# Head steps every 12 tiles and own products every 5 tiles in the second gather stage

## The reference

```python
xn = layernorm(x)
# graph part: mean of the neighbours' rows, and the node's own row
agg  = segment_sum(xn[nbr], dst);  mean = agg / max(count, 1)
gnn  = xn @ W1.T + b1 + mean @ W2.T + b2
# mixing part: 8 heads of 32 columns
k = headnorm(xn) * kw + kb;  v = headnorm(xn) * vw + vb      # std with ddof=1
kv = einsum('nd,ne->de', k, v) / N                            # per head
mix = xn_heads @ kv + xn
x = x + gnn + mix
# experts: top-1 routing with a capacity, two matmuls with relu, scattered back
x = x + ffn(layernorm(x))
```

## Time and profile before

| | |
|---|---|
| median of 3 runs | 2139.8 us (2136.44 to 2140.73) |
| the profiled execution | 2139.9 us, span 2138.3 us |
| busy: PE / DVE / ACT / POOL | 75% / 65% / 34% / 48% of the span |
| 880 gathers on POOL (L439) | 894.3 us busy |
| `experts`, last block | from about 1671 us on |

### The profile page before, as it was taken

How to read it: one execution, slowest core, us unless ns; L and a number is a source line. 1 busy time by engine, 2 the same in 40 slices (tenths; PEclk the granted TensorE clock), 3 DMA queues, 4 the chain that set the end, 5 groups by cost and what they waited for, 6 DMA issues and landing times. The chain is left out here.

```text
span 2138.3 us, 26245 instructions
## 1 busy us (share of the span) xinstructions
PE 1593.7 (75%) x6551; PEld 889.5 (42%) x6551; DVE 1387.2 (65%) x4056; ACT 721.3 (34%) x2020; POOL 1036.1 (48%) x1021
## 2 busy tenths in 40 slices
PE   4666887677878777365555658888676699999997
PEld 3552332233333333022222224554365466666665
DVE  7568998789999998366656555555465144444444
ACT  3336997004877776000000001111064122222221
POOL 2001001777777777777777777777425111111111
PEclk9788999767999999555555557667555799999999
DMA  5117000333333333933333344444844422222200
GB/s 167 40 40 295 31 0 15 100 101 96 94 97 97 99 97 99 99 110 103 103 101 103 102 114 130 123 121 128 102 155 168 133 89 89 97 92 92 91 23 5
DMA packets 89183, 210.70 MB, mean 99 GB/s; under 512 B 20627, under 2 KB 49849, under 8 KB 86081
## 3 DMA queue, kind: packets, MB, share of 16 engines
q0 software_dynamic: 51888, 138.08, 24.8%
q1 hardware_dynamic: 35496, 70.56, 9.7%
q10 hardware_dynamic: 1680, 0.67, 0.2%
HBM read 163.98 MB, written 49.89 MB: 100 GB/s over the span
## 5 line engine op out<-in xcount | busy, mean ns | idle before, releaser
L902 DVE TENSOR_TENSOR XA<-XA,bank 128x257 f32 x880 | 369.0, 419 | 345.0 <-PE bank L657 319.5
L439 POOL DMA_INDIRECT G<-xn_parts,idx x440 | 443.0, 1007 | 277.7 <-DVE srcl L994 143.9
L439 POOL DMA_INDIRECT w<-xn_parts,idx x440 | 451.3, 1026 | 134.1 <-issue 134.1
L656 PE MATMUL bank<-G,S 128*128 128x257 f16 x440 | 154.8, 352 | 165.2 <-DMA G<-xn_parts,idx 140.4
L1582 POOL DMA_INDIRECT out<-ob,tok x64 | 66.6, 1040 | 401.7 <-DVE ob L1568 399.0
L656 PE MATMUL bank<-w,S 128*128 128x257 f16 x440 | 152.6, 347 | 138.8 <-DMA w<-xn_parts,idx 124.0
L529 ACT ACTIVATE LV<-LH,v 125x128 f16<-125x128 f16 x600 | 182.9, 388 | 189.5 <-DVE LH L1063 189.2
L1506 PE MATMUL bank<-w,ht 128*117 128x256 f32 (+1 forms) x1024 | 223.7, 379 | 0.0
L1495 PE MATMUL bank<-xt,w 128*128 128x468 f32 (+1 forms) x512 | 215.3, 579 | 0.8 <-ACT xt L1520 0.8
L1506 PEld LDWEIGHTS bank<-w,ht 128*117 128x117 f32 (+1 forms) x1024 | 188.8, 186 | 30.5 <-issue 0.4
L1530 ACT ACTIVATE ht<-bank,b1c 128x468 f32<-128x468 f32 (+1 forms) x128 | 85.7, 670 | 333.8 <-PE bank L1495 333.8
(11 more groups left out here) (225 smaller groups left out, 2542.9 us busy)
## 6 DMA issues: line engine op xcount, KB each, us to landing
w<-f SPq DMA_DIRECT2D x16, 1024.0 KB, 7.4
expert_rows<-G SPq DMA_DIRECT2D x7, 2048.0 KB, 21.3
xb<-expert_rows SPq DMA_DIRECT2D x8, 1028.0 KB, 11.4
xb<-expert_rows SPq DMA_DIRECT2D x8, 939.7 KB
G<-xn_parts,idx POOLq DMA_INDIRECT x440, 2.8
w<-xn_parts,idx POOLq DMA_INDIRECT x440, 2.8
XA<-x SPq DMA_DIRECT2D x6, 1024.0 KB, 5.7
xn_parts<-G POOLq DMA_DIRECT2D x12, 512.0 KB, 3.7
```

Of the source, the lines that this page charges most:

```text
L439: pool.indirect_dma_start(g[:, o:o + 2 * D], None, tab, bass.IndirectOffsetOnAxis(ap=idx[:, t:t + 1], axis=0)).then_inc(s_g[t % RING], 16)
L656: pe.matmul(psA[t % AR][:, 0:AGW], lhs, g[:, o + D:o + 2 * D + 1], start=True, stop=True)
L902: v.tensor_tensor(XA[:, ds(o, AGW)], XA[:, ds(o, AGW)], psA[t % AR][:, 0:AGW], ALU.add).then_inc(s_ev, 1)
```

## The change

The work and its order on each engine are the same; the tiles that it stands behind differ. Head steps come every `HS` = 12 tiles from tile 16 on, with VectorE's steps behind tiles s = 0 to 9 of the twelve as before, and TensorE's six pieces in two halves, three behind s = 10 and three behind s = 11. `KV_AT` and `OWN0` are now counted in tiles: 16 + 12 x 17 = 220. Own products start every `OS` = 5 tiles, with the transposes behind tile 0 and the matmuls behind tile 2 of the five; the last starts at tile 460, and VectorE's last add for it stands behind tile 465.

```diff
--- before.py
+++ after.py
@@ -77,9 +77,11 @@
 
 T0 = CHUNKS[0][3]
 COLS0, COLS1 = CHUNKS[0][1], CHUNKS[1][1]
-HEAD0, KV_AT = 1, 1 + NB // HD + 1
+HS, OS = 12, 5
+HEAD0 = GR
+KV_AT = HEAD0 + HS * (NB // HD + 1)
 OWN0 = KV_AT
-assert len(CHUNKS) == 2 and OWN0 * GR + 4 * NB < CHUNKS[1][3] and NB % LD == 1 and COLS1 % LB == 0
+assert len(CHUNKS) == 2 and OWN0 + OS * NB < CHUNKS[1][3] and NB % LD == 1 and COLS1 % LB == 0
 
 
 RB0, RB1 = 2, 4
@@ -741,8 +743,8 @@
         for h in range(2):
             pe.matmul(psG[h][:, 0:KW], zero32[:, :], W1[:, 0:KW], start=True, stop=False, skip_group_check=True)
         for t in range(T0, TILES):
-            g, s = (t - T0) // GR, (t - T0) % GR
-            if g == KV_AT and s == 0:
+            u = t - T0
+            if u == KV_AT:
                 for h in range(2):
                     ins = pe.matmul(psG[h][:, 0:KW], zero32[:, :], W1[:, 0:KW], start=False, stop=True,
                                     skip_group_check=True)
@@ -754,13 +756,16 @@
                               stop=True).then_inc(s_se, 1)
                 pe.wait_ge(s_kv, 1)
             sum_tile(t)
-            if HEAD0 <= g < KV_AT and s >= 10:
-                m, pieces = g - HEAD0, (HD if g - HEAD0 < NB // HD else 1) * 2
-                if s == 10:
+            m, s = (u - HEAD0) // HS, (u - HEAD0) % HS
+            if HEAD0 <= u < KV_AT and s >= HS - 2:
+                pieces = (HD if m < NB // HD else 1) * 2
+                if s == HS - 2:
                     pe.wait_ge(s_kn, m + 1)
-                products(m, range(min(s - 10, pieces), min(s - 9, pieces)), pieces - 1)
-            if OWN0 <= g and s % 2 == 0 and (g - OWN0) * LD + s // 4 < NB:
-                own((g - OWN0) * LD + s // 4, s % 4)
+                half = pieces // 2
+                products(m, range(0, half) if s == HS - 2 else range(half, pieces), pieces - 1)
+            b, s = (u - OWN0) // OS, (u - OWN0) % OS
+            if OWN0 <= u and s in (0, 2) and b < NB:
+                own(b, s)
 
     @block.vector
     def _(v):
@@ -1158,14 +1163,15 @@
             v.tensor_tensor(XA[:, xcols(b)], XA[:, xcols(b)], xr[b % LD], ALU.add).then_inc(s_x0, 1)
 
         for t in range(T0, TILES):
-            g, s = (t - T0) // GR, (t - T0) % GR
-            if g == KV_AT and s == 0:
+            u = t - T0
+            if u == KV_AT:
                 key_values()
             tile(t)
-            if HEAD0 <= g < KV_AT and s < 10:
-                heads(g - HEAD0, s, HD if g - HEAD0 < NB // HD else 1)
-            b = (g - OWN0) * LD + s // 4 - 1
-            if OWN0 <= g and s % 4 == 0 and 0 <= b < NB:
+            m, s = (u - HEAD0) // HS, (u - HEAD0) % HS
+            if HEAD0 <= u < KV_AT and s < HS - 2:
+                heads(m, s, HD if m < NB // HD else 1)
+            b, s = (u - OWN0) // OS - 1, (u - OWN0) % OS
+            if OWN0 <= u and s == 0 and 0 <= b < NB:
                 own(b)
```

## The result

The changed kernel took 2148.3 us in the median of 16 runs (2141.06 to 2154.85), beside 2139.4 us for the kernel before in the same session (16 runs). The ratio is 1.0042, with a 95% interval from 1.0029 to 1.0055: slower by 0.4%, about 9 us. The profiled execution has a span of 2151.4 us against 2138.3. It took 2153.1 us, 4.7 above the median of its kernel, while the one before (2139.9) lies on its median, so the two profiles are 13.1 us apart and the medians 8.9.

A forecast was written before the change was run, and what follows sets the result against it. GpSimd's issue of 880 gathers was taken to bound both gather stages, with transfers setting the tail. Terms -0.5 (x loads) + 0 (key-value step) + 2.7 (heads) + 4.4 (own products) = +6.6 us gave 2146 us, range 2133 to 2158.

The forecast's parts named there:

- What bounds the kernel: Both gather stages: issuing 880 gathers on GpSimd sets their length, the other engines work in its shadow; transfers set the tail.
- Own products out of the tail: End of the second gather stage: six blocks' products leave the last 24 tiles, worth nothing to the end.
- The term for the x loads: Tail of the second gather stage: moving the x loads out gives -0.5 us, bounds 0 and -1.3.
- Key-value step: Moved from tile 288 to tile 220, it holds TensorE 5.6 us at the sum and costs the same: 0.
- Heads in 12 tiles: Head stage: lumps of three pieces put VectorE out of phase, more gathers lengthened; +2.7 us, bounds -0.5 and +6 (+12 with jitter).
- Own products in 5 tiles: Tiles 220 to 460: L881 goes through all five places, 30 x 0.49 us against 10.3; +4.4 us, bounds 0 and +12.5.
- The sum: Whole kernel: -0.5 + 0 + 2.7 + 4.4 = +6.6 us, forecast 2146 us.
- The signs named beforehand: GpSimd gaps at most 0.31 us; gathers over 0.98 us (head), about 1.01 (own); last sum about 15 us behind last issue.
- C: Rival, faster: the tail is TensorE's, so removing products there takes 11.6 us off, 2128 us; chance 0.07.
- D: Rival, faster: with period 5 most L881 fall free at 0.15 us each, own stage loses 4.5, 2133.5 us; chance 0.13.
- E: Rival, slower: the ring fills, GpSimd stops and own products show at 0.5 us per block, +25 us, 2165 us; chance 0.05.
- B: Rival, no change: collisions keep their rate per L881 or are unrelated to VectorE; 2139.3, up to 2144 us; chance 0.27.

## Why the prediction was right, point by point

- **What bounds the kernel.** Right, and shown: GpSimd has no gap over 0.31 us in the profile after, and in the old schedule taking 43 us out of the gathers' lengths and 13 out of the tail took 55 us out of the span.
- **Own products out of the tail are worth nothing.** Right. Leaving them out altogether, x loads included, shortens the tail by 2.8 us; moving them shortened it by 2.2. The term for the x loads, -0.5 us with a bound of -1.3, was too small by 1.7 us if all of it is theirs; the runs did not part it from what the products gave.
- **Key-value step.** Right: 5.5 us of waiting at the sum, and no gap on GpSimd.
- **Heads in 12 tiles.** The mechanism was right and can be followed in the profile after, the size was not. L886 behind a step's last tile is late by 0.47 us in the median of the eight places, as forecast, and costs 0.34 us, not 0.42. The gather that it lengthens then makes one meet L1106 at seven of eight, 0.61 us each, where the forecast had 0.74 or nothing. All the same +2.7 us was forecast, with 6 as the bound and 12 with jitter, and +6.8 was measured. The term had a wrong base: 7.1 us is the loss of 256 tiles, and the whole stage of 272 loses 10.0. On that base the forecast 9.8 would have been no change, and 16.8 is 7.0 above it. Of these 7.0, 4.1 are L1106 in steps for which the forecast had no collision: 2.2 at three places where the add comes 0.2 us earlier at 2.4 GHz, and 1.8 at four where VectorE is late. I took the head stage as wholly at 1.2 GHz and had worked out the other level for the own products alone. The rest is spread over L1121 (0.9 us), L886 and L1106 behind it. With one profile of each kernel and the stage's scatter (1.5 to 10.0 us in three profiles with the old head steps), these shares are rough. Whether the lumps are needed for the loss with landings on time no run tests; the runs without them had late landings.
- **Own products in 5 tiles.** +4.4 us forecast, 14.7 against 10.3; +3.1 measured, 13.9 against 10.8. The value of 0.49 us for each L881 is close to the 0.46 that 13.9 us over 30 of them give. That is also today's rate (0.47): the term comes from more L881 standing beside own products, 30 in place of 22, more than from the places within the five tiles.
- **The sum.** +6.6 us forecast, +8.9 us in the medians, +13.1 us between the two profiled spans, of which some 3 us are the first stage's and the start's scatter. That the sum came so near is in part luck: the head steps' term was 4.1 us too small, the own products' 1.3 too large, and the tail gave back 1.7 us more than forecast. The signs named beforehand hold: the gathers average 1.03 us in the head stage and 1.01 in the own stage.
- **The rule of the Trainium skill** (SBUF — State Buffer, "Who interferes with whom"), an inference there, that a tensor_tensor with two SBUF inputs does not stall a DMA because descriptor generation needs only the write interface, does not hold for these indirect DMAs: with one of L881's inputs moved to PSUM and its length unchanged, the gathers lost 42.0 us less. The same section has such an instruction contend with a GpSimd instruction that reads SBUF; a gather takes its indices from SBUF (`idx`), so the page's two sentences may both be true, but no run here tries this beside a DMA from GpSimd that has no indices. That page's other sentence, that an instruction with at most one SBUF input outside the two-port modes doesn't contend, agrees with the 101 gathers beside L887 that take no more than 0.98 us.
- **The rivals.** C fell with the run without the last products. D fell: L886 costs 0.46 us, not 0.15. E did not occur on the chips of the result. B described the two chips with late landings, by a cause I had not named: there the ring is full and a lengthened gather costs nothing.

## What to carry to other kernels

Where GpSimd's descriptor work sets the pace, look at how long its instructions take and what VectorE runs beside them before moving any other work: the position of one VectorE instruction relative to a gather is worth up to 1 us each time, and one collision delays the gathers behind it into the next. Take the collision away (one operand in PSUM) rather than tune the phase, and let padding read different rows. Ask of every phase that you work out at one clock what it is at the other, since the schedule itself can move it: the head stage's granted clock is 0.58 to 0.60 in all eight profiles with steps of 12, and 0.50 to 0.52 in the four with steps of 16 and landings on time.

## What the runs showed of the hardware that was not expected

- A gather that begins inside a tensor_tensor with two SBUF inputs ends 0.82 us behind it (1020.17 to 1020.99). With the first input in PSUM the same instruction, still 1.22 us, left the gathers alone: 20.7 us lost in the first stage became nothing.
- A tensor_scalar of 0.34 us on half-precision data with one input tensor in SBUF (L1073) lengthens them too: 50 of the 115 gathers that begin inside it in the profile after, ending 0.82 us behind it in the median, 10.6 us in all. No run parts it from what stands beside it.
- 128 lanes reading one 1 KB row of HBM arrive 1.78 us apart and fill the engines at 0.89; reading 128 different rows they keep up with GpSimd's 1.25 us, at a share of 0.32.
- The same program takes 2138 us on some chips and 2281 us on two others. There the transfers of GpSimd's queue land so late that 32 outstanding gathers are not enough, with the engines' share no higher (0.32 in the head stage, against 0.35). What delays them stays open.
